# A row's maximum in four pieces: VectorE in the feed-forward stage of a two-layer gated cross-attention block

## The reference, cut to what matters

```python
def activation_quant(x):
    scale = 127.0 / jnp.clip(jnp.max(jnp.abs(x), axis=-1, keepdims=True), 1e-05, None)
    return jnp.clip(jnp.round(x * scale), -128, 127) / scale

def weight_quant(w):
    scale = 1.0 / jnp.clip(jnp.mean(jnp.abs(w)), 1e-05, None)
    return jnp.clip(jnp.round(w * scale), -1, 1) / scale

def bitlinear(x, w):
    return jnp.einsum('bsh,oh->bso', activation_quant(x), weight_quant(w))

x_norm = rmsnorm(x, norm_weight)                 # rows of 512
gate_up = bitlinear(x_norm, w_gate_up)           # 512 -> 2 * 1408
gate, up = jnp.split(gate_up, 2, axis=-1)
hidden = jnp.square(jax.nn.relu(gate)) * up      # rows of 1408
return bitlinear(hidden, w_down)                 # 1408 -> 512
x = x + jnp.tanh(g_ffn[1]) * (the above of layernorm(x))
```

## Time and profile before

| | us |
|---|---|
| median of 3 runs | 3244.68 |
| lowest and highest run | 3242.96, 3249.32 |
| the profiled execution's own time | 3239.97 |
| its span, first to last instruction | 3238.1 |
| busy PE, DVE, ACT, POOL | 2945.6, 2383.7, 2087.5, 1362.2 |

### The profile page before, as it was taken

One profiled execution on the slowest core, in us unless ns is written; L12 is line 12 of the kernel. 1 busy time (PEld: TensorE's weight loads), 2 busy tenths in 40 slices (PEclk: granted clock), 3 DMA queues, 4 the chain that ended last, 5 costly groups with the idle time before them and its releaser, 6 DMA issues. The chain is left out here.

```text
span 3238.1 us, 56526 instructions
## 1 busy us (share of the span) xinstructions
PE 2945.6 (91%) x15414; PEld 2368.8 (73%) x15414; DVE 2383.7 (74%) x4704; ACT 2087.5 (64%) x4271; POOL 1362.2 (42%) x1691
## 2 busy tenths in 40 slices
PE   6869998897999979879999899999999999899777
PEld 4546666675888867768877688888888888688543
DVE  6769998864767668767666189999999999626376
ACT  3458887421666546556666488888888888433354
POOL 3412000403000076256666277777777777441121
PEclk9989999898999989989999999999999999999999
DMA  5797664216878669856566523322333222486200
GB/s 188 213 250 172 156 149 115 82 36 208 279 249 280 209 228 269 212 152 180 164 180 191 193 68 96 96 89 76 97 96 94 74 93 70 143 267 218 77 24 30
DMA packets 427934, 491.09 MB, mean 152 GB/s; under 512 B 53812, under 2 KB 285140, under 8 KB 427764
## 3 DMA queue, kind: packets, MB, share of 16 engines
q1 hardware_dynamic: 414804, 436.50, 45.6%
q0 software_dynamic: 12960, 52.61, 4.8%
HBM read 312.69 MB, written 176.31 MB: 151 GB/s over the span
## 5 line engine op out<-in xcount | busy, mean ns | idle before, releaser
L2824 POOL TENSOR_SCALAR h_probs<-h_exp,h_rowsum_inv 128x512 f32<-128x512 f32 x512 | 355.7, 695 | 275.9 <-PE h_pT L2672 259.3
L2752 DVE TENSOR_REDUCE h_neg_max<-h_scores 128x1 f32<-128x512 f32 x512 | 349.3, 682 | 141.5 <-PE h_scores L2664 141.3
L2714 ACT ACTIVATE h_exp<-h_scores,h_neg_max 128x512 f32<-128x512 f32 x512 | 355.7, 695 | 109.2 <-DVE h_neg_max L2752 100.7
L2765 DVE TENSOR_TENSOR h_probsT_lo<-h_pT,h_probsT_hi 128x512 fp32r<-128x512 f32 x512 | 348.4, 681 | 0.0
L2672 PE MATMUL h_pT<-ident,h_probs 128*128 128x128 f32 x2048 | 306.3, 272 | 0.9 <-POOL h_probs L2824 0.8
L2672 PEld LDWEIGHTS h_pT<-ident,h_probs 128*128 128x128 f32 x2048 | 252.9, 139 | 69.7 <-POOL h_probs L2824 1.8
L2723 ACT CAST h_probsT_hi<-h_pT 128x512 fp32r<-128x512 f32 x512 | 301.1, 588 | 0.9 <-PE h_pT L2672 0.9
L2940 PE MATMUL k_acc<-k_w_hi,k_cat 128*128 128x512 f32 x512 | 201.3, 393 | 11.6 <-POOL k_w_lo L3021 10.8
L2687 PE MATMUL h_pO<-h_probsT_hi,n_lo 128*128 128x512 f32 x512 | 201.5, 393 | 0.0
L2941 PE MATMUL k_acc<-k_w_lo,k_cat 128*128 128x512 f32 x512 | 200.7, 392 | 0.0
L901 ACT ACTIVATE b_probs<-b_scores,b_neg_max 128x512 f32<-128x512 f32 x256 | 179.8, 702 | 24.2 <-DVE b_neg_max L928 24.2
(11 more groups left out here) (445 smaller groups left out, 9072.3 us busy)
## 6 DMA issues: line engine op xcount, KB each, us to landing
e_w_raw<-in_w SPq DMA_DIRECT2D x24, 1792.0 KB, 8.0
lnT<-g_out SPq DMA_DIRECT2D x160, 256.0 KB, 2.3
n_raw<-lnT SPq DMA_DIRECT2D x64, 512.0 KB, 5.3
e_w_raw<-in_w SPq DMA_DIRECT2D x24, 896.0 KB, 9.9
n_raw<-lnT SPq DMA_DIRECT2D x64, 256.0 KB, 5.5
n_raw<-v SPq DMA_DIRECT2D x64, 256.0 KB, 5.8
cat<-h_cat SPq DMA_DIRECT2D x128, 128.0 KB, 1.8
k_cat<-cat SPq DMA_DIRECT2D x128, 128.0 KB, 4.6
```

The source lines that it names most:

```text
L2714: nc.scalar.activation(Pr[:, r % 4], pS[r % 2][:], ACT.Exp, bias=nmax[:, r % 4:r % 4 + 1], accum_out=rsum[:, r % 4:r % 4 + 1]).then_inc(ex ...
L2752: v.tensor_reduce(nmax[:, r % 4:r % 4 + 1], pS[r % 2][:], axis=AX, op=ALU.max, negate=True).then_inc(nmax_done.sem, 1)
L2765: v.tensor_tensor(PTl[:, br * HPG + h, :, bass.ts(q, P)], pT[r % 4][:], PTh[:, br * HPG + h, :, bass.ts(q, P)], ALU.subtract).then_inc(lo_ ...
L2824: nc.gpsimd.tensor_scalar(Pn[:, r % 4], Pr[:, r % 4], rinv[:, r % 4:r % 4 + 1], 1.0, ALU.mult, ALU.mult).then_inc(norm_done.sem, 1)
```

## The change

A new stage `quarter_max` takes the maximum of each quarter of `Hd` one step behind its product, into a tile of four numbers per row. `hidden_scale` then takes the maximum over these four instead of over 1408. Only DVE's instructions change in kind or number; the tiles of four numbers, one more semaphore and 64 instructions are new.

```diff
+    amq = m.sb("amax_quarters", [P, 2, CH])
...
+        def quarter_max(i, r):
+            n, b, c = tile(i, r)
+            dve.wait_ge(hd.sem, hd.done(i * N + r))
+            if c == 0:
+                dve.wait_ge(amd2.sem, amd2.free(n))
+            v.tensor_reduce(amq[:, b, c:c + 1], Hd[:, b, c * CW:(c + 1) * CW], axis=AX, op=ALU.max,
+                            apply_absolute_value=True).then_inc(amqd.sem, 1)
+
         def hidden_scale(n, b):
             c = slice(b, b + 1)
-            dve.wait_ge(hd.sem, hd.depth + (n + 1) * CH)
-            v.tensor_reduce(am2[:, c], Hd[:, b], axis=AX, op=ALU.max, apply_absolute_value=True).then_inc(amd2.sem, 1)
+            dve.wait_ge(amqd.sem, amqd.depth + (n + 1) * CH)
+            v.tensor_reduce(am2[:, c], amq[:, b], axis=AX, op=ALU.max).then_inc(amd2.sem, 1)
...
-        pipeline(dve, N, N, [(at(3, residual), 17), (at(3, hidden_scale), 10), (at(3, hidden_round), 11), (at(3, hidden_int), 12),
-                             (at(3, round_add), 3), (at(3, round_sub), 4), (hidden, 9), (at(3, scale), 1)])
+        pipeline(dve, N, N, [(at(3, residual), 17), (quarter_max, 10), (at(3, hidden_scale), 10), (at(3, hidden_round), 11),
+                             (at(3, hidden_int), 12), (at(3, round_add), 3), (at(3, round_sub), 4), (hidden, 9), (at(3, scale), 1)])
```

More of the change, by code:

```diff
@@ L3101, in l1_ffn @@
     tr2, qTd, down, fod, x4d = (m.flag(s) for s in ("tr2", "qT", "dn", "fo", "x4"))
-    gu, rl, sq, hd = m.flag("gu"), m.flag("rl"), m.flag("sq"), m.flag("hd")
+    gu, rl, sq, hd, amqd = m.flag("gu"), m.flag("rl"), m.flag("sq"), m.flag("hd"), m.flag("amq")
     block = m.block()
```

## The result

The changed kernel took 3248.44 us (median of 20 runs, 3240.51 to 3253.14) against 3241.93 us for the kernel before (20 runs): the ratio is 1.0014, 95% interval 1.0008 to 1.0020, which on 3241.93 us is +4.5 us, 2.6 to 6.5. The prediction said 3248.3 us. The change costs a little over a thousandth, inside the 0.2% that the prediction called no change. A second set of 12 runs on another occasion gave 1.0008 (0.9994 to 1.0022), +2.6 us, and alone would not tell the two kernels apart.

The account below looks back on a forecast made before the run. Bound: a loop of 6.97 us on DVE and 4.00 us on PE and ACT. Fourteen blocks at +0.215 (3.0), ramp 0.5 and tail 0.1 gave +3.6 us, thus 3248.3 us, range 3242 to 3254.

Parts of the forecast that it names:

- The loop: DVE from c3 to `k_xi`, 6.97 us, then PE and ACT to the next c3, 4.00 us: period 10.97.
- Sum per block: Net change on DVE's part of the loop: -0.895 at the head, +0.555 at c0 and at c1, +0.215 us in all.
- The head: Start of `hidden_scale` on DVE: 1.64 us becomes 0.745 with c3's piece and the small maximum, -0.895.
- P: Length of one piece, a maximum over 352 columns on DVE: 0.515 us, bounds 0.401 and 0.552.
- The price of a wait: On DVE, waiting for the result of the instruction just ahead costs 0.12 us more.
- The piece of c2: Behind the residual, ahead of c3: 3.84 us after `k_xi` against ACT's 4.00, so it costs nothing.
- Ramp: Ahead of the first maximum, pieces of c0 and c1 stand before a `k_xi`, mostly beside ACT waits: +0.5 us.
- Tail: Last two blocks: c2's piece uncovered, +0.4 each; with the other terms 0.8 + 0.215 - 0.895 = +0.1 us.
- Sum: Whole kernel: 3.0 for fourteen blocks, 0.5 ramp and 0.1 tail, +3.6 us.
- the likeliest case: The forecast itself, 3248.3 us, given 64% with its own range of 3245 to 3251.
- Rival 3: PE's clock falls in each block after the merged 1.92 us gap, transposes 0.61: 1.35 a block, 19.5 us, 3264; 7%.
- Rivals 1, 2 and 4: 1: free waits or short pieces, about 3243, 14%; 2: dearer pieces, 3251.1, 12%; 4: both gains together, 3236.5, 3%.

Follow-up runs that it names:

- The spare piece: Kernel before plus an unused maximum over 352 columns: of c0 ahead of the rounding (on the loop), ratio 1.0026; of c2 behind its product (beside it), 1.0004.
- the moved pieces: Changed kernel with the pieces of c0 and c1 one instruction later, behind the rounding and `hidden_int`: period 10.91 us, ratio 0.9996.
- the kernel with three pieces in the gap: Changed kernel with the pieces of c0, c1 and c2 moved behind the product c2, where DVE idles: period 10.06 us, ratio 0.9948.

## Why the prediction was right, step by step

- *The loop*: right. The spare piece costs 0.56 us on it and nothing beside it.
- *Sum per block*: +0.215 forecast, +0.19 measured in all four profiles. The head gained 0.92 instead of 0.895, since the piece of c3 is 0.50 long, not 0.515. P came from two other shapes of the same operation and was 2 ns off the mean.
- *The price of a wait*, 0.12: right, by the moved pieces (0.25 for two).
- *The piece of c2*: it costs nothing in a normal block, as said: c3 starts 0.03 us after ACT's square ends. In a low block it stands on the loop.
- *Ramp*: forecast +0.5, right in one profile of four and too small in three. From the first `k_xa` to the first `k_clipped_max` it is 17.34 and 17.44 us before and 17.82 in three profiles of the changed kernel, 16.92 in one. With the 0.92 gained at its head that is about +1.4 and once +0.5; in the three, one more product of the ramp runs at the low clock (four gate and up products of 1.36 to 1.38 us, against three in the other one and before).
- *Tail*: the last two periods are 10.14 and 9.18 instead of 9.56 and 8.60, +0.58 each; the forecast's terms give 0.4 + 0.215 = 0.615. The final eleven down products differ between profiles of one kernel: 3.89 and 4.85 us before, 2.55, 4.11, 4.88 and 4.08 in the changed kernel.
- *Sum*: forecast +3.6, measured +4.5 timed (+2.6 in the second set) and +4.4 in the means of four and two profiles of the stage. By parts, the forecast's terms put where they fall:

| part of the stage | forecast, us | measured, us |
|---|---|---|
| to the first `k_clipped_max` | 0.5 - 0.9 = -0.4 | +0.2 |
| first period | +0.2 | +0.4 (12.06 - 11.70) |
| twelve in the middle | +2.6 | +2.3, and +0.9 by the three low blocks of one profile |
| last two periods | +1.2 | +1.2 |
| behind the last maximum | 0 | -0.5 |

The steady part is as forecast. The rest goes mostly with PE's clock, by 2 us and more from one profile to another, so that its tenths prove nothing. That the sum came out within 1 us is partly luck: the clock's share was set at nothing in the likeliest case.

- *The time itself*: 3248.3 was said and 3248.44 measured, and that closeness is luck. The forecast stood on a median of 3 runs, 3244.68, where 20 runs gave 3241.93, and the difference of the two medians, 6.5 us, is larger than the ratio's 4.5.
- *Rival 3*: a block with a low clock costs about what it said (1.35 forecast; 12.19 to 12.53 instead of 10.97 seen, 1.22 to 1.56), and by the path through the residual. The make-up is another: it took the transposes as low and they still took 0.40; instead two down products took 1.06 instead of 0.59. And it befell 3 of 48 middle blocks and not all, 0.9 us a run by these profiles, not the 19.5 of the rival. Its cause, the gap of 1.92, is not shown for the middle, since 45 blocks with that gap kept the full clock. Transposes of 0.61, its sign, are seen at the start of the stage and in first blocks, before as after, and in no middle block of the changed kernel.
- *Rivals 1, 2 and 4*: out, by the period, the length of the pieces and the price of the waits.

## What to carry to other kernels

Find the loop first, and ask of each piece of a split operation on which side of it the piece comes to stand. Splitting a reduction so that its last piece is short shortens the path to its result (by 0.92 us here), but the pieces that were to be early stood on the same loop with a fixed cost each and a stall behind their product; in the engine's idle gap the same pieces cost nothing and the split is worth 0.5%. And on DVE put another instruction between a producer and its consumer: it gave back 0.12 us for each such pair here.

## What else the runs showed

A one-number product of POOL takes five times as long when it starts beside DVE's rounding of 1408 columns. It is shown here in the kernel before, in the changed kernel, where it runs beside a piece, and in the kernel with three pieces in the gap, where it is beside the rounding again:

```profile
3130.44 0.93 POOL L3286 TENSOR_TENSOR k_cube<-k_cube 128x1 f32<-128x1 f32 x1
```

```profile
3133.95 0.19 POOL L3295 TENSOR_TENSOR k_cube<-k_cube 128x1 f32<-128x1 f32 x1
```

```profile
3106.96 0.93 POOL L3303 TENSOR_TENSOR k_cube<-k_cube 128x1 f32<-128x1 f32 x1
```

0.93, 0.19 and 0.93 us. The kernel before with the spare piece on the loop, where nothing is new but that piece ahead of the rounding, has 0.19 us as well. So the length goes with the neighbour on DVE; why the rounding slows POOL and the piece doesn't, no run shows. POOL is not on the loop, so it costs nothing here.
